# Four transformer layers on one core: a DMA transposes layer 1's probabilities, its scores are made pair by pair, and the norms elsewhere take one product

## The reference, cut to what matters

```python
def _fq(x, delta, zp, n_bits):                     # layer 1
    xi = _round_ste(x / delta) + zp
    xq = jnp.clip(xi, 0.0, 2.0 ** n_bits - 1.0)
    return (xq - zp) * delta
...
    sim = jnp.einsum('bhid,bhjd->bhij', _fq(q, dq, 128.0, 8), _fq(k, dk, 128.0, 8)) * SCALE
    attn = jax.nn.softmax(sim, axis=-1)
    out = jnp.einsum('bhij,bhjd->bhid', _fq(attn, dw, 0.0, 8), _fq(v, dv, 128.0, 8))
...
def _ln(x, g, b):                                  # layers 1 to 3; layer 0 has no mean
    mu = jnp.mean(x, -1, keepdims=True)
    var = jnp.var(x, -1, keepdims=True)
    return (x - mu) * jax.lax.rsqrt(var + EPS) * g + b
```

## Time and profile before

| what | before |
|---|---|
| median of 3 runs | 5082.05 us (5082.00 to 5082.79) |
| profiled execution, its own time | 5084.24 us |
| its span, first to last instruction | 5082.1 us |
| mean granted TensorE clock | 0.97 |
| busy: PE, PEld | 4750.2 us (93%), 3575.8 us (70%) |
| busy: DVE, ACT, POOL | 2947.2 us (58%), 2834.6 us (56%), 2125.3 us (42%) |
| chain that ended last | PE 79%, ACT 9%, POOL 8%, DVE 2%, issue 2% |
| DMA | 103.09 MB, mean 20 GB/s |

### The profile page before, as it was taken

One profiled execution on the slowest core, in us unless ns is written; L12 is line 12 of the kernel. 1 busy time (PEld: TensorE's weight loads), 2 busy tenths in 40 slices (PEclk: granted clock), 3 DMA queues, 4 the chain that ended last, 5 costly groups with the idle time before them and its releaser, 6 DMA issues.

```text
span 5082.1 us, 91660 instructions
## 1 busy us (share of the span) xinstructions
PE 4750.2 (93%) x34496; PEld 3575.8 (70%) x34496; DVE 2947.2 (58%) x6697; ACT 2834.6 (56%) x9058; POOL 2125.3 (42%) x4307
## 2 busy tenths in 40 slices
PE   8999999977878777889999999999999999999998
PEld 5666666656666666667777777777777777887777
DVE  5555555556665656664444445444445777677765
ACT  4555555688888888873333333333333666666664
POOL 2333333487787878771111111111112444444443
PEclk9999999989898988999999999999999999999999
DMA  2000000000000000001000000000000000000000
GB/s 81 20 20 23 20 24 23 24 27 20 11 21 14 17 18 14 18 30 39 14 11 14 14 14 11 14 14 14 11 22 24 33 21 18 21 18 17 21 16 7
DMA packets 40040, 103.09 MB, mean 20 GB/s; under 512 B 4912, under 2 KB 21552, under 8 KB 38192
## 3 DMA queue, kind: packets, MB, share of 16 engines
q1 hardware_dynamic: 39600, 97.23, 5.9%
HBM read 82.53 MB, written 14.68 MB: 19 GB/s over the span
## 4 chain that ended last, share of the span: by engine, by line
PE 79%; ACT 9%; POOL 8%; DVE 2%; issue 2%; DMA 0%; SPq 0%; ACTq 0%; DVEq 0%
PE ring L1268 47%; PE ring L1219 11%; PE score L1200 10%; ACT e L1378 5%; POOL e L1735 4%; PE ring L1250 3%; PE ring L1243 3%; POOL e L1745 2%; PE ring L1257 2%; PE ring L1216 1%; DVE nmax L1513 1%; POOL rsumw L1728 1%; POOL work L1721 1%; ACT probs L1418 1%; PE score L1195 1%
## 5 line engine op out<-in xcount | busy, mean ns | idle before, releaser
L1738 POOL TENSOR_SCALAR e<-e,rsum 112x375 f32<-112x375 f32 (+1 forms) x2048 | 1080.8, 546 | 2611.6 <-DVE rsum L1520 2606.2
L1418 ACT COPY probs<-ring 125x336 f32<-125x336 f32 (+1 forms) x997 | 413.0, 448 | 1530.3 <-PE ring L1219 1470.5
L1513 DVE TENSOR_REDUCE nmax<-score 112x2 f32<-112x750 f32 (+1 forms) x1152 | 1057.2, 950 | 328.2 <-PE score L1200 327.6
L1378 ACT ACTIVATE e<-score,nmax 112x375 f32<-112x375 f32 (+1 forms) x2048 | 1038.7, 539 | 88.3 <-DVE nmax L1513 86.5
L1268 PE MATMUL ring<-h,weights 128*128 128x224 f32 x3840 | 903.4, 370 | 5.5 <-ACT h L1350 3.0
L1268 PEld LDWEIGHTS ring<-h,weights 128*128 128x128 f32 x3840 | 712.2, 197 | 77.7 <-issue 27.0
L1219 PEld LDWEIGHTS ring<-consts,e 112*125 112x125 f32 x4608 | 594.0, 189 | 231.1 <-issue 172.8
L1200 PE MATMUL score<-keys,q 64*112 64x375 f32 (+2 forms) x3584 | 559.1, 491 | 162.8 <-ACT e L1378 150.6
L1219 PE MATMUL ring<-consts,e 112*125 112x112 f32 x4608 | 659.9, 279 | 9.3 <-POOL e L1738 4.8
L1378 ACT ACTIVATE e<-score,nmaxc,quant 112x375 f32<-112x375 f32 (+1 forms) x1024 | 555.1, 554 | 10.7
L1268 PE MATMUL ring<-weights,ctx 128*125 128x256 f32 (+1 forms) x1536 | 551.2, 488 | 0.1
(11 more groups left out here) (120 smaller groups left out, 5858.7 us busy)
## 6 DMA issues: line engine op xcount, KB each, us to landing
ctx<-ctx_t SPq DMA_DIRECT2D x128, 375.0 KB, 2.9
out_t<-x SPq DMA_DIRECT2D x64, 224.0 KB, 1.9
x<-out_t SPq DMA_DIRECT2D x48, 224.0 KB, 2.5
weights<-weights SPq DMA_DIRECT2D x7, 1024.0 KB, 5.6
x<-x_t SPq DMA_DIRECT2D x16, 224.0 KB, 2.5
weights<-weights SPq DMA_DIRECT2D x1, 3328.0 KB, 12.0
weights<-weights SPq DMA_DIRECT2D x1, 2304.0 KB, 9.1
weights<-weights SPq DMA_DIRECT2D x1, 2048.0 KB, 7.2
```

What stands on the lines that cost most here:

```text
L1378: ins = nc.scalar.activation(e_of(u)[:, n * width:(n + 1) * width], score_bank(u)[0:S, n * width:(n + 1) * width], ACT.Exp, bias=minus, sc ...
L1418: ins = nc.scalar.copy(dst, src)
L1513: ins = dve.tensor_reduce(to, src, AX, ALU.max, negate=True)
L1738: ins = nc.gpsimd.tensor_scalar(mine, mine, rsum[0:S, slot(u), n:n + 1], 0.0, ALU.mult, ALU.add)
```

## The change

Layer 1, the probabilities. `weigh` stops after L1735. A new DVE step, `eight`, takes both units of a pair at once, cuts them at 255, takes the rounding number off and writes bfloat16 to a new buffer, `steps`, with four slots. A new SP step, `flip`, issues one transposing DMA for each pair from `steps` into `probs`: 112 rows of 6 blocks of 128 columns for a cross pair and of 8 for a self pair. `turn` and its `save` are gone from layer 1. `exp` now waits for the `eight` of the pair four before, `eight` for the `flip` of the layer 1 pair four before, `flip` for the `pv` of the octet two before, and `pv` for the octet's flips.

Layer 1, the scores. Layer 1 leaves `QUADS`: its scores are made pair by pair, and wait for the exp of the pair two before alone. The chunks of its keys become 128, 128 and 119 rows, not 3 times 125.

The norms of layers 0, 2 and 3. POOL adds the two feature blocks (`fold` of x, `foldsq` of the squares, `cfold` of the context's squares), and the mean or variance is then one matmul, not two. The planner has new costs, which changes the order of the lists in all layers.

```diff
-QUADS = (0, 1, 2, 3)
+QUADS = (0, 2, 3)
...
-                by = "V" if o.layer == 1 else "VA"
-                self.turn_of[u] = self.job(p.index + lag + 0.1 * i, "turn", o.layer, o.s, o.b, 0, by, u)
+                if o.layer != 1:
+                    self.turn_of[u] = self.job(p.index + lag + 0.1 * i, "turn", o.layer, o.s, o.b, 0, "VA", u)
...
-                self.pv_of[o] = self.job(p.index + lag + 0.5, "pv", ...
+                self.pv_of[o] = self.job(p.index + (3.4 if o.layer == 1 else lag + 0.5), "pv", o.layer, o.s, o.b, o.half, PV_BY[o.layer], o)
...
-            self.add("weigh", p, "G", (2.7 if own else 1.15) + ((1.4 if own else 1.3) if q else 0), p.index + 1.0)
+            self.add("weigh", p, "G", (2.7 if own else 1.15) + (0.3 if q else 0), p.index + 1.0)
+            if q:
+                self.add("eight", p, "V", 1.0 if own else 0.85, p.index + 1.6)
+                self.add("flip", p, "D", 2.5, p.index + 1.8)
...
+            if n.layer > 1:
+                self.add("fold", n, "G", 0.5, self.mean_of[n].pos - 0.4)
+            if n.layer != 1:
+                self.add("foldsq", n, "G", 0.5, j.pos - 0.4)
...
+            self.add("cfold", b, "G", 0.7, j.pos - 0.4)
...
+        steps = sb("steps", [P, STEPSLOTS, 8 * P], BF16)
...
-            wait.saves([plan.turn_of[u] for p in o.pairs for u in p.units])
+            if layer == 1:
+                for p in o.pairs:
+                    flip_done(wait, p)
+            else:
+                wait.saves([plan.turn_of[u] for p in o.pairs for u in p.units])
...
+                wait.wait_ge(folded, nth["fold", j.norm])
+                return pe.matmul(ps[:, 0:N], mean_w[:, :], squares[:, j.norm.index % 2, 0, :], start=True, stop=True)
...
+                wait.wait_ge(ctx_folded, nth["cfold", j.b])
+                return pe.matmul(ps[:, 0:T], mean_w[:, :], ctx_sq[:, 0, :], start=True, stop=True)
...
-                wait.done([plan.turn_of[u] for u in plan.pairs[p.index - ES // 2].units])
+                before = plan.pairs[p.index - ES // 2]
+                if before.octet.layer == 1:
+                    wait.wait_ge(stepped, nth["eight", before])
...
+                elif kind == "eight":
+                    p = x_
+                    wait.wait_ge(weighed, nth["weigh", p])
+                    i = plan.nth_of_one[p]
+                    if i >= STEPSLOTS:
+                        flip_done(wait, plan.ones[i - STEPSLOTS])
...
+                    dve.tensor_scalar(to, src, ROUND + 255.0, ROUND, ALU.min, ALU.subtract).then_inc(stepped, 1)
...
+            nc.gpsimd.memset(steps[:, :, :], 0.0).then_inc(consts_made, 1)
...
+                if kind == "foldsq":
+                    wait.wait_ge(squared, nth["square", x_])
+                    to = squares[:, x_.index % 2, 0, :]
+                    nc.gpsimd.tensor_tensor(to, to, squares[:, x_.index % 2, 1, :], ALU.add).then_inc(squares_folded, 1)
...
-                if o.layer == 1:
-                    wait.wait_ge(weighed, nth["weigh", p])
-                    full = count_of(o) * width
-                    for u in p.units:
-                        ins = nc.gpsimd.tensor_scalar(steps_of(u)[:, 0:full], e_of(u)[:, 0:full], 1.0, -ROUND,
-                                                      ALU.mult, ALU.add)
-                    ins.then_inc(stepped, 1)
...
+                elif kind == "flip":
+                    p = x_
+                    n = nth["flip", p] - 1
+                    wait.wait_ge(stepped, nth["eight", p])
+                    wait.done([plan.pv_of[o] for o in plan.probs_before(p.octet)])
+                    sp.dma_start(flipped(p), steps_of(p), transpose=True).then_inc(turned[n % FLIPS], 16)
```

More of the change, by code:

```diff
@@ L222, in place_attention @@
         self.turn_of, self.pv_of = {}, {}
+        self.ones = [p for p in self.pairs if p.octet.layer == 1]
+        self.nth_of_one = {p: i for i, p in enumerate(self.ones)}
         for p in self.pairs:
@@ L342, in tensor_cost @@
         if j.kind == "turn":
-            if j.layer == 1:
-                return 0.19 if j.of.octet.attn == "cross" else 0.25
             return 0.35 if j.of.octet.attn == "cross" else 0.42
@@ L465, in before @@
             if x.index >= ES // 2:
-                for u in self.pairs[x.index - ES // 2].units:
-                    yield "job", self.turn_of[u]
+                if self.pairs[x.index - ES // 2].octet.layer == 1:
+                    yield "eight", self.pairs[x.index - ES // 2]
+                else:
+                    for u in self.pairs[x.index - ES // 2].units:
+                        yield "job", self.turn_of[u]
+        elif kind == "eight":
+            yield "weigh", x
+            i = self.nth_of_one[x]
+            if i >= STEPSLOTS:
+                yield "flip", self.ones[i - STEPSLOTS]
+        elif kind == "flip":
+            yield "eight", x
+            for o in self.probs_before(x.octet):
+                yield "job", self.pv_of[o]
         elif kind == "invert":
@@ L487, in before @@
                 yield "job", self.var_of[self.norms[x.index - 2]]
+        elif kind == "fold":
+            yield "x", (x.layer, x.s)
+            for i in self.residual(self.mean_of[x]):
+                yield "save", i
+            if x.index >= 2:
+                yield "job", self.var_of[self.norms[x.index - 2]]
+        elif kind == "foldsq":
+            yield "square", x
+        elif kind == "cfold":
+            yield "csquare", x
         elif kind == "scale":
@@ L540, in before_job @@
             for p in o.pairs:
-                for u in p.units:
-                    yield "save", self.turn_of[u]
+                if o.layer == 1:
+                    yield "flip", p
+                else:
+                    for u in p.units:
+                        yield "save", self.turn_of[u]
             for i in self.value_jobs(o):
@@ L894, in four_layers @@
         stepped = sem("stepped")
+        turned = [sem(f"turned_{i}") for i in range(FLIPS)]
         zeroed = sem("zeroed")
```

131 lines of the change are left out of this document (90 added, 41 removed).

## The result

| what | before | after |
|---|---|---|
| median of the runs | 5082.02 us (5081.56 to 5082.79) | 5000.31 us (4997.47 to 5003.12) |
| ratio | | 0.9839, 95% interval 0.9822 to 0.9856 |
| span of the profiled execution | 5082.1 us | 5000.1 us |
| mean granted TensorE clock | 0.97 | 0.957 |

A forecast was written before the change was run, and what follows sets the result against it. The prediction took PE to bound layers 0, 2 and 3, and a chain of waits between engines, with none full, layer 1. From 5082 us it took 163 for layer 1 and 89 for norms: 4830 us, range 4765 to 4950.

The forecast's parts named there:

- Norms, layers 0 and 2: Layers 0 and 2: PE is the bound, so dropped norm matmuls are gained nearly whole, 29 and 27 us.
- Norms, layer 3: Layer 3: 40.3 us of norm matmuls go, taken at 0.82 for PE's share of the chain, 33 us gained.
- Rival 3: Norms of layers 0, 2 and 3 give nothing, as folds arrive late at PE; total 4919 us; chance 0.05.
- Layer 1, the work of each engine: Layer 1, per stream: PE 51.4 to 54.6 us, POOL 48 or less, DVE 49, ACT 66.7.
- So ACT becomes the bound of layer 1.: Layer 1: ACT's 66.7 us a stream is the floor, with PE, DVE and POOL at 55 us or less.
- of 14.2 us idle I keep 4.3: Layer 1: of ACT's 14.2 us idle a stream only 4.3 stay, so the period falls 10.9 us to 71.
- the 88% that I had named as a sign of being wrong: Layer 1: ACT under 88% busy would show the forecast wrong; over 92% busy would show it right.
- Rival 2: Layer 1: flips become the bound at 4.8 us cross, 6.4 self, 106 us a stream with other traffic; 5354 us; chance 0.07.
- the microsecond that I had allowed: Layer 1: no PE wait for flips beyond a microsecond was a sign of the forecast being right.
- Rival 1: Layer 1: path from self pair to next cross scores stays 44.4 us; period 77.5, total 4927 us; chance 0.25.
- Rival 4: Layer 1 gives nothing, as the cost-made order misfits and PE or DVE waits in new places; 4993 us; chance 0.03.
- my 71 us: Layer 1: forecast period of a stream, 10.9 us less than before, giving -163 us over 15 periods.

The follow-up runs named there:

- norms_only: The kernel before with only the folds of layers 0, 2 and 3 and their planner steps; 5021.67 us, ratio 0.9880 against the kernel before.
- old_exp_costs: The changed kernel with the planner's cost of an exp outside layer 1 as before; 4981.32 us, ratio 0.9796 against the kernel before.
- short_self_exps: The changed kernel with three of four exps of a layer 1 self unit and their sums left out; 4959.77 us.
- either_saves: old_exp_costs with layer 1's quantised saves (k, q, v, ck, cv) open to DVE as well as ACT; 4904.69 us, ratio 0.9647 against the kernel before.
- no_flips: old_exp_costs with no flip issued from layer 1's third stream on; 4959.78 us.
- two_flips: The changed kernel with each flip issued twice, the second into a spare buffer, each waiting for the pair before; 5088.64 us.

## Why the prediction was right in two layers and wrong in two

- **Norms, layers 0 and 2.** Nearly right: -26.0 and -25.0 us for -29 and -27, and partly by luck. The folds alone gave 20 and 19; some 4 us in each came from the new exp cost. A single matmul costs more than half of two: 0.396 us a record for 0.360 with the context's 375 columns, 0.279 for 0.235 with 224, so by these records PE saves 1.7 us a stream in layer 0, not 1.86. In norms_only PE also waits 6.4 us of 60 to 900 us for POOL's weighing, where it waited 2.6 before, so the folds are not wholly covered there; in the change that wait is gone. A fold takes POOL 0.66 us for x, 0.70 for squares and 1.09 for the context's squares in the change, within the 0.3 to 1.1, but 1.6 for the last in norms_only.
- **Norms, layer 3 (-33, was +5.8).** The size of the step was nearly right: layer 3 is 27 us shorter than before in norms_only and 25 in old_exp_costs. What failed is that I costed the planner's other new numbers at nothing. I had written that they change the order in all layers, and put a price on none. The new exp cost took the whole gain back, 30 us (old_exp_costs). Rival 3 (the folds arrive late at PE) is not how it went: norms_only has the same folds and the gain.
- **Layer 1, the work of each engine.** Mostly right. ACT 66.75 us (66.7), DVE 48.7 (49), POOL 47.9 (48 or less); `eight` 0.575 and 0.687 us (0.6). PE was mis-sized: 60.6 us for 51.4 to 54.6. By 1300 to 2000 us of both, a stream lost 12.7 us of transposes, but the scores grew by 4.2 (cross ones to 6.3, as the upper bound said; self ones, which I left out, from 0.8 to 1.9). pv grew by 1.0, the means of x by 0.7 and, over ten streams of each, the products of `weights,ctx` by 2.2 us a stream, while those of `heads,weights` fell by 1.0 and those of `h,weights` by 1.5. The granted clock of that stretch is 0.85 for 0.90 before; how much of this it explains no run separates.
- **"So ACT becomes the bound of layer 1."** This is the step that failed, with "of 14.2 us idle I keep 4.3". I struck out ACT's waits one by one and took the fullest engine as the period. The waits for maxima did go, and others came: ACT waits for PE, and PE for ACT, across the self pairs. short_self_exps shows it: 7.6 us less of ACT gives 2.8. After either_saves it gives nothing. ACT was 83% busy, below the 88% that I had named as a sign of being wrong.
- **What stood in the way of the pairs.** They cost 3.0 us a stream alone, were worth 1.3 with the flips, and 4.15 with free saves as well. What I missed is a condition: PE must have an empty ring bank while ACT does exps. I had read from the code that PE's results go to a ring of four, and not who empties it. The profile before did not show it as a wait on a save, since there PE's idle time stood before scores and transposes. But it showed the place. I read PE's 8.2 us before scores as the price of quads, and in order of time 7.1 of them are one stand, right behind the self exps:

```profile
1702.24 0.56 PE L1200 MATMUL score<-keys,q 32*112 32x375 bf16 x4 [7.09 <-ACT e L1378]
```

There ACT had two table loads and the gate's pass to do (4.3 us from 1693.79 on) before it came to the cross exps. Of the two pairs that the quad waits for, the first was done at 1699.83 and the second at 1702.19, so the quad itself accounts for at most 2.4 of the 7.1 us. In the changed kernel PE stands before cross scores inside the self exps instead, 3.95 and 3.92 us, and 1.06 behind them.

- **The flips.** Estimated at 0.65 us of the engines and 2.5 us to land; measured 1.01 and 2.7. All of their way costs 1.6 us a stream (no_flips), which I had at nothing, and PE's two waits for them, 1.4 and 1.7 us a stream, are above the microsecond that I had allowed. Rival 2 was to decide from 4.4 us each (4.2, if the 4.1 us of other traffic are counted, as its 106 us do); at 1.01 it was far. The Trainium skill's "VectorE: DVE Perf Modes", section "The three transpose paths", gives 1309 ns for a 128x128 block by DMA. It does not say that blocks follow each other, though the prediction put that on the page. Here six or eight blocks land in 2.7 us and hold the engines for 1.01, so the measurement decides against it. The 261 GB/s of the Trainium skill's "DMA: Bandwidth & Descriptors", section "Latency and other measured facts", which it gives for a non-contiguous middle dimension, is nearer: 183.5 KB of the mean flip in 1.01 us are 182 GB/s.
- **Rival 1** (the path from a self pair to the next cross scores holds) gave 77.5 us and 4927 us in all. Its place was right, the stretch across the self pairs, but its chain was not: it was to end at ACT's q, and in the changed kernel no PE wait ends there. **Rival 4** (layer 1 gives nothing, because of the order) at 4993 us came nearest, and had 0.03. That is a coincidence of the sum: layer 1 gave 37 us, and it was layer 3 that gave nothing.

The sum once more, by what the runs show: norms in layers 0 and 2 -51 us; layer 3 +6, where 25 less was to be had; layer 1 -37 for -163. In layer 1 the change missed my 71 us by 8.5. With the saves open to DVE and the old exp costs 4.9 of them come (3.8 of which the kernel before would have gained too), with the flips left out as well 5.3 in all. The other 3.2 us, 48 in 15 periods, stay open. There no engine is above 85% busy, and a lighter ACT or PE hardly helps, so the work of neither is the cause. POOL and DVE were never made lighter, and POOL's weighing has 13.4% of the chain in either_saves, so POOL stands as an untested rival. That the time is handed round between all four is argued from the chain and not shown by a run. Three other orders were tried, and each was worse.

## What to carry to other kernels

An engine is not the bound because it is the fullest. Before its floor is taken as the new period, ask of each wait that is struck out what the waiting engine's partner needs at that moment, and who alone can give it: here a free ring bank, which only the engine that was busy with exps could empty. Open such a duty to a second engine before, or together with, the change that leans on it (here 3.8 us a stream before, 5.05 after). And where a list of costs sets the order, each changed number is an edit with a price of its own: the one exp cost took 30 us in layer 3, for some 8 gained elsewhere.

## What was not expected of the hardware

A transposing DMA took its issuing queue longer than a plain one. On SP in order of time, around the flips of one stream (start us, us, what):

```profile
1441.95 0.35 SPq L1883 DMA_DIRECT2D out_t<-x  x1
1443.94 0.33 SPq L1872 DMA_DIRECT2D x<-out_t  x1
1444.32 1.21 SPq L1878 DMA_TRANSPOSE probs<-steps  x1
1445.81 0.33 SPq L1893 DMA_DIRECT2D ctx<-ctx_t  x1
```

A plain load or store took 0.33 to 0.35 us to issue here, a flip 1.21. In two_flips, with 40 a stream, SP's issuing of them (SPq) is 4.5% of the chain of waits over 1300 to 2000 us.

TensorE's clock fell with its stands. From 1455.0 to 1485.7 PE was busy for 51% and was granted 0.72. Eight matmuls of 224 columns took 1.78 us at 1458.22, and 3.36 at 1485.70, behind waits of 3.95, 3.92 and 1.06 us: nearly twice as long. The granted clock tells why. It was 0.66 from 1474.0 to 1485.7, where PE was busy for 2.1 of 11.7 us, 0.50 (the level of 1.2 GHz) in the 3.4 us behind, where PE was full, and 1.00 (that of 2.4) from 1495 on:

```profile
1474.00:1485.70 11.70, 2.11 (x23) 0.79 (x15) 6.63 (x17) 11.44 (x46) 8.17 (x20) 0.66 0.18 35
1485.70:1489.10 3.40, 3.40 (x16) 2.64 (x20) 1.70 (x5) 2.72 (x8) 3.31 (x5) 0.50 0.01 1
```

So part of what idle time seems to offer PE is taken again in the work after it: the means of x cost 0.442 us a matmul in that stream, and 0.358 in layer 1 of the kernel before.
